# A gated cross-attention block: another order of its opening on five engines

## The chip, the cores and the metric

One core of a Trainium2 chip runs the whole program. The metric is device microseconds of one execution; the time before is a median of 490.72 us over 3 runs (490.58 to 491.27). TensorE multiplies, VectorE and ScalarE read its results out of PSUM, GpSimd works in SBUF alone, and DMA queues are fed from SyncE and ScalarE. Each engine works through its own list in order, and the engines meet at semaphores.

## The reference, cut to what matters

Eight batches of 512 rows by 256 channels go through a local attention (AFT) with a context, a feed-forward block and a second gated block.

```python
emb = x + pos_encod          # x is the context here, pos_encod the layer-normed x
q, k, v = emb @ wq + bq, emb @ wk + bk, emb @ wv + bv
w = pos_bias * (abs(i - j) < 64)
ek = exp(k - max_over_rows(k));  ew = exp(w - max_over_columns(w))
y = sigmoid(q) * (ew @ (ek * v)) / (ew @ ek)
a = layer_norm(y @ wo + bo + emb) * gamma + beta
r = layer_norm(relu(a @ w1 + b1) @ w2 + b2 + a)
x1 = x + tanh(g_xattn) * r
out = x1 + tanh(g_ffn) * gated_ffn(layernorm(x1))
```

## The kernel before, in words

Every matrix product is made of three: each operand is split into a rounded part (`_hi`, made on ScalarE) and the rest (`_lo`, made on VectorE or GpSimd), and hi·hi, lo·hi and hi·lo are added up in PSUM. So one 256x256 projection of a batch is 12 matmuls of 512 columns (`channels_out`, L1173) or 24 of 256 (`rows_out`, L1190).

The work is software-pipelined over the batches. An opening takes batch 0 to the end of its attention and into its hidden layer and prepares batch 1; seven steps (`run_steps`, L274) follow, each for three batches at different stages; a tail ends it. All orders are written out by hand, one list for each engine, and a list's next instruction waits in place if its semaphore is not there yet.

Weights come in units of 1024 columns through four staging buffers: unit 0 is keys and queries, unit 1 values and output projection, units 2 and 3 are w1, 4 and 5 w2, 6 and 7 the second block. `unit_high(u)` rounds on ScalarE, `unit_low(u)` makes the rest on VectorE or GpSimd; a unit's buffer can be loaded anew from SyncE only after its `unit_low`.

What the change touches, in the order of the opening:

- TensorE waits for the identity (L1388), then for the embedding of batch 0, turns it, and does `keys(0)` and `queries(0, 3)`; it turns the exponentials of the position bias, then those of the keys (`turn_keys`), then the masks of the far columns (L1416), and does `values(0, 3)`.
- `weigh_first` (L1297) makes the denominator, `weigh` (L1266) with part 1 the numerator. Far columns are summed by tiles: the sums go to PSUM, ScalarE rounds them (`sums_high`), VectorE makes the rest (`sums_low`), and TensorE takes them up again for the second half of the numerator. `weigh` can place other work (`between`) just ahead of the wait for these sums.
- `turn_emb(1, 1)` (L1228) turns the embedding of batch 1 between the two. ScalarE's `emb_high(1)` and a copy of it into `xk` (L1070, L1071) come ahead of `sums_high(0, 1)` (L1072) in its list.
- `fold_beta` (L1314) multiplies beta with w1, 16 products of one column, and needs w1 as loaded.
- Then the output projection, `keys(1)`, `queries(1, 3)`, the turn of the normalised rows, two quarters of the hidden layer, `values(1)`, `turn_keys(1)` and `add_hidden(0, 0)`. TensorE waits for `w_lo_done[5]` (L1448) just ahead of step 1.
- VectorE's list: `recip` (one for each of two chunks, with `sums_low(0, 1)` between them, L798), `make_y`, `make_b1`, `y_low`, `unit_low(2)`, `first_attention_sum` (L804) and so on to `keep_values(1)` (L819).
- GpSimd's list ends with `unit_low(4)`, `emb_plus_bo(1, 1)`, `unit_low(5)` (L463), `stats("mid", 0)`, `scale_a`, `stats("head", 2)` and `make_emb(pool, 2, 0)` (L467).
- ScalarE's list ends with `exp_keys(1)`, `a_high(0)`, `exp_q(1, 3)`, `normalise("head", 2, x_in)` (L1082), `hidden_high(0, 0)`, `hidden_high(0, 1)` (L1084) and `ek_high(1)`.
- SyncE's list has the loads of units 6 and 7 (L356), each behind the `unit_low` that frees its buffer, and behind them the loads for later batches.

Of the kernel before, what the change touches and what calls it, by code (L numbers as in the profile page):

```python
# [7 lines left out]
ALU = mybir.AluOpType  # L8
# [3 lines left out]
P = 128  # L12
# [16 lines left out]
NU = 8  # L29

# [12 lines left out]
def flamingo_gated_block(nc, A_x, A_ctx, A_vec, A_rows, A_far, A_pos, A_wk, A_wq, A_wv, A_wo,  # L43
# [14 lines left out]
    with ctx:  # L58
# [321 lines left out]
        def _(pool):  # L380
# [75 lines left out]
            stats("head", 1)  # L456
            emb_plus_bo(0, 0)
# [4 lines left out]
            emb_plus_bo(1, 1)  # L462
            unit_low(5)  # L463
# [3 lines left out]
            make_emb(pool, 2, 0)  # L467
            pool.wait_ge(dve_const, 4)
# [39 lines left out]
        def _(dve):  # L508
# [269 lines left out]
            unit_low(0)  # L778
            pos_max(0)
            emb_low(0)  # L780
            pos_max(1)
            head_stats(1)
            key_max(0)
            unit_low(1)
# [15 lines left out]
            make_y(0)  # L800
            make_b1()
            y_low(dve, 0)
            unit_low(2)
# [3 lines left out]
            unit_low(3)  # L807
            a_low(0)
            head_stats(2)
            sum_keys(1)  # L810
            hidden_low(0, 0)
# [5 lines left out]
            dve.tensor_scalar(gates[:, 1:2], gates[:, 2:3], 0.5, None, ALU.mult).then_inc(dve_const, 1)  # L817
            hidden_low(0, 1)
            keep_values(1)  # L819
# [81 lines left out]
        def _(act):  # L901
# [140 lines left out]
            for u in range(2):  # L1042
# [4 lines left out]
                if u == 0:  # L1047
                    unit_high(1)
            act.wait_ge(c_col_done, 1)
            act.activation(c_col, pos_nmax, ACT.Exp).then_inc(c_col_done, 1)  # L1050
            exp_keys(0)
            act.wait_ge(act_const, 1)
            exp_q(0, 3)
            act.wait_ge(far_landed, 16)
            act.wait_ge(c_col_done, 2)
            for a in range(TT):
                v = tile(far_in, TT + a, FAR)
                act.activation(v, v, ACT.Identity, scale=c_col[:, a:a + 1]).then_inc(far_masked, 1)
# [19 lines left out]
            normalise("mid", 0, res)  # L1078
            exp_keys(1)
            a_high(0)  # L1080
            exp_q(1, 3)
            normalise("head", 2, x_in)  # L1082
            hidden_high(0, 0)
            hidden_high(0, 1)  # L1084
            ek_high(1)
# [62 lines left out]
        def _(pe):  # L1148
# [165 lines left out]
            def fold_beta():  # L1314

                for k in range(DC):
                    pe.wait_ge(unit_landed[W1_UNITS[k]], unit_count(W1_UNITS[k]))
                for m in range(HC):
                    for k in range(DC):
                        last = mm(bank(3, 0)[:, m:m + 1], stage[UNIT_STAGE[W1_UNITS[k]]][:, m * P:(m + 1) * P],  # L1320
                                  vec[:, C_BETA + k:C_BETA + k + 1], m == 0 and k == 0, m == HC - 1 and k == DC - 1)
# [239 lines left out]
```

## Time and profile before

| what | value |
|---|---|
| median of 3 runs | 490.72 us |
| profiled execution | 490.83 us |
| its span, first to last instruction | 489.1 us |
| TensorE matmuls busy | 454.1 us, 93% of the span |
| VectorE | 394.0 us, 81% |
| GpSimd | 257.0 us, 53% |
| ScalarE | 239.9 us, 49% |

Busy time is an average over the whole span. Matmuls are pipelined and overlap in the rows, so the time of a group of matmuls is read from the start of its first to the start of what follows. In a timeline each row has a start and a length in us (of merged neighbours together, with their count behind the x), the engine, the line, the operation and the tile written and read; in brackets stands how long the engine was idle before it and what ended that.

### The profile page before, as it was taken

Reading aid. Unit: us, or ns where it says so; the run is one execution under the profiler, and the core shown is the slowest. Engines: PE = TensorE matmul, PEld = TensorE weight load, DVE = VectorE, ACT = ScalarE, POOL = GpSimd, SP = SyncE. Lnnn points to the kernel's source line nnn. Section 1 sums busy time; section 2 is a strip of 40 time slices with the busy share of each in tenths; the row PEclk is TensorE's granted clock in tenths of the full one; section 3 lists DMA queues with packets and bytes.
Section 4 is the critical chain, followed back from the end, with each engine's and each line's share of the span. In section 5 each row is a group of like instructions: output and inputs, shape, how many; then the busy total and the mean of one; then the engine's idle time right before and its main releaser. Section 6 shows DMA issues by size and latency. Waiting matters only on the chain.

```text
span 489.1 us, 8042 instructions
## 1 busy us (share of the span) xinstructions
PE 454.1 (93%) x3010; PEld 412.2 (84%) x3010; DVE 394.0 (81%) x725; ACT 239.9 (49%) x371; POOL 257.0 (53%) x230
## 2 busy tenths in 40 slices
PE   1889989989999999999999999999999998989776
PEld 1789789879989898989989898989889997979765
DVE  4899869987959979598959988698939974795967
ACT  2773373646265634645274644645263634446323
POOL 3657413671587536962497446952494247551510
PEclk9997999999999999999999999999999999999959
DMA  7740410012002300112002200111001100020002
GB/s 260 257 129 2 151 43 1 2 44 87 1 0 76 100 0 1 29 58 88 1 0 88 88 1 1 44 43 44 1 1 44 44 1 1 7 81 1 1 0 87
DMA packets 21894, 23.35 MB, mean 48 GB/s; under 512 B 992, under 2 KB 20960, under 8 KB 21856
## 3 DMA queue, kind: packets, MB, share of 16 engines
q1 hardware_dynamic: 20768, 21.26, 13.3%
q10 hardware_dynamic: 1088, 1.57, 0.9%
q8 instruction: 24, 0.39, 0.3%
q14 instruction: 14, 0.11, 0.1%
HBM read 18.64 MB, written 4.19 MB: 47 GB/s over the span
## 4 chain that ended last, share of the span: by engine, by line
PE 50%; issue 16%; POOL 14%; DVE 14%; ACT 4%; DMA 2%; POOLq 0%; DVEq 0%; ACTq 0%
PE ps L1150 46%; DVE y L611 4%; POOL hid_lo L219 3%; POOL xk_lo L219 2%; PE ps L1156 2%; DVE xk L679 2%; POOL a_rows L402 2%; DMA x<-in_pos 1%; PE ps L1165 1%; DVE y L608 1%; POOL ev_lo L219 1%; POOL x_beta L402 1%; DVE hid_lo L760 1%; ACT xk_hi L975 1%; DMA x_in<-in_x 1%
## 5 line engine op out<-in xcount | busy, mean ns | idle before, releaser
L1150 PE MATMUL ps<-w_hi,hid_hi 128*128 128x256 f32 x320 | 79.8, 286 | 2.7 <-DVE y L618 1.7
L760 DVE SCALAR_TENSOR_TENSOR hid_lo<-ps,neg_b,hid 128x512 fp32r<-128x512 f32 x64 | 44.1, 739 | 43.4 <-ACT hid L1020 43.4
L1150 PE MATMUL ps<-w_lo,hid_hi 128*128 128x256 f32 x320 | 78.4, 282 | 0.0
L1150 PEld LDWEIGHTS ps<-w_hi,hid_hi 128*128 128x128 f32 x320 | 60.3, 189 | 5.5 <-DVE y L618 3.7
L1150 PEld LDWEIGHTS ps<-w_lo,hid_hi 128*128 128x128 f32 x320 | 60.2, 188 | 0.2
L611 DVE RECIPROCAL y<-y 128x512 f32<-128x512 f32 x16 | 53.7, 3353 | 0.5
L1150 PE MATMUL ps<-a_hi,w_hi 128*128 128x512 f32 x128 | 50.8, 397 | 1.6 <-ACT a_hi L1003 1.6
L1014 ACT ACTIVATE hid_hi<-ps,b 128x512 fp32r<-128x512 f32 x64 | 40.5, 685 | 23.5 <-PE ps L1150 23.5
L1150 PE MATMUL ps<-a_hi,w_lo 128*128 128x512 f32 x128 | 50.8, 397 | 0.0
L1150 PE MATMUL ps<-w_hi,hid_lo 128*128 128x256 f32 x320 | 45.6, 284 | 3.5 <-DVE hid_lo L760 2.3
L219 POOL TENSOR_TENSOR ev_lo<-res,ev_hi 128x1024 fp32r<-128x1024 f32 x8 | 19.1, 2384 | 56.0 <-ACT ev_hi L963 56.0
L1150 PEld LDWEIGHTS ps<-w_hi,hid_lo 128*128 128x128 f32 x320 | 41.0, 188 | 5.1 <-DVE hid_lo L760 2.7
L1020 ACT ACTIVATE hid<-hid_hi,neg_b 128x512 f32<-128x512 f32 x64 | 42.7, 723 | 0.0
L219 POOL TENSOR_TENSOR hid_lo<-xr,hid_hi 128x1024 fp32r<-128x1024 f32 x7 | 16.8, 2403 | 37.7 <-ACT hid_hi L979 37.7
L1150 PE MATMUL ps<-a_lo,w_hi 128*128 128x512 f32 x128 | 35.1, 396 | 0.0
L1150 PEld LDWEIGHTS ps<-a_hi,w_hi 128*128 128x128 f32 x128 | 24.1, 188 | 7.0 <-issue 2.0
L402 POOL TENSOR_TENSOR a_rows<-norm,gamma_rows 128x1024 f32<-128x1024 f32 x8 | 19.8, 2471 | 19.4 <-issue 17.0
L1150 PEld LDWEIGHTS ps<-a_lo,w_hi 128*128 128x128 f32 x128 | 24.0, 188 | 6.0 <-DVE a_lo L744 0.2
L1150 PEld LDWEIGHTS ps<-a_hi,w_lo 128*128 128x128 f32 x128 | 24.1, 188 | 5.1
L1150 PE MATMUL ps<-emb_hi,w_hi 128*128 128x512 f32 x64 | 27.0, 421 | 1.2 <-ACT emb_hi L933 1.2
L1150 PE MATMUL ps<-emb_hi,w_lo 128*128 128x512 f32 x64 | 26.3, 410 | 0.0
L979 ACT ACTIVATE hid_hi<-xr 128x1024 fp32r<-128x1024 f32 x7 | 7.4, 1061 | 36.2 <-DVE xr L679 36.2
(216 smaller groups left out, 1285.9 us busy)
## 6 DMA issues: line engine op xcount, KB each, us to landing
x_in<-in_x SPq DMA_DIRECT2D x8, 512.0 KB, 4.5
emb<-in_ctx SPq DMA_DIRECT2D x8, 512.0 KB, 3.5
x_beta<-in_x SPq DMA_DIRECT2D x8, 512.0 KB, 3.6
out<-out_sb SPq DMA_DIRECT2D x7, 512.0 KB, 2.9
hid<-in_w SPq DMA_DIRECT2D x2, 512.0 KB, 4.4
x<-in_pos ACTq DMA_DIRECT2D x1, 512.0 KB, 6.4
out_sb<-in_pos ACTq DMA_DIRECT2D x1, 512.0 KB, 7.3
x<-in_w SPq DMA_DIRECT2D x1, 512.0 KB, 5.8
```

Of the source, the lines that this page charges most:

```text
L219: eng.tensor_tensor(dst, src, f32(hi), ALU.subtract).then_inc(done, 1)
L402: pool.tensor_tensor(dst.rearrange("p (a d) -> p a d", a=TT), src.rearrange("p (a d) -> p a d", a=TT), r, op).then_inc(done, 1)
L608: dve.scalar_tensor_tensor(out=tile(y, c, T), in0=tile(gate_q, c, T), scalar=1.0, in1=bank(1, c), op0=ALU.add, op1=ALU.mult).then_inc(den_ ...
L611: dve.reciprocal(tile(y, c, T), tile(y, c, T)).then_inc(recip_done, 1)
L679: dve.scalar_tensor_tensor(out=tile(dst, c, T), in0=tile(delta_buf(n), c, T), scalar=vec[:, mu + c:mu + c + 1], in1=xn_t[:, c * (T + 1):c ...
L760: dve.scalar_tensor_tensor(out=tile(hid_lo[q % 2], b, T), in0=bank(HP[q], b), scalar=neg_b1[:, m:m + 1], in1=tile(hid[q % 2], b, T), op0=A ...
L975: act.activation(tile(xk_hi, c, T), tile(xk, c, T), ACT.Copy).then_inc(xk_hi_done, 1)
L979: act.activation(xr_hi, xr_of(n), ACT.Copy).then_inc(xr_hi_done, 1)
L1014: act.activation(tile(hid_hi[q % 2], b, T), bank(HP[q], b), ACT.Relu, bias=b1[:, m:m + 1]).then_inc(hid_hi_done, 1)
L1020: act.activation(tile(hid[q % 2], b, T), f32(tile(hid_hi[q % 2], b, T)), ACT.Identity, bias=neg_b1[:, m:m + 1]).then_inc(hid_shifted, 1)
L1150: return pe.matmul(o, s, m, start=start, stop=stop, skip_group_check=True)
L1156: last = pe.transpose(bank(dst, c)[:, a * P:(a + 1) * P], src[:, D * a + c * P:D * a + (c + 1) * P], ident)
```

## The change

The lists of TensorE, VectorE, ScalarE and GpSimd for the opening are put into another order; 24 products of the identity with itself are added ahead of the first embedding; the beta products are placed between the products of the second batch's keys; and the far masks go from ScalarE to GpSimd. SyncE's list and the seven steps keep their code.

```diff
+WARM = 24
@@ GpSimd
             stats("head", 1)
+            pool.wait_ge(far_landed, 16)
+            pool.wait_ge(c_col_done, 2)
+            for a in range(TT):
+                v = tile(far_in, TT + a, FAR)
+                pool.tensor_scalar(v, v, c_col[:, a:a + 1], None, ALU.mult).then_inc(far_masked, 1)
             emb_plus_bo(0, 0)
             make_emb(pool, 1, 1)
             ev_low(0)
             low(pool, emb_lo, xk, emb_hi, emb_raw_done, 1, emb_lo_done)
             unit_low(4)
-            emb_plus_bo(1, 1)
-            unit_low(5)
             stats("mid", 0)
             scale_a(0, 0)
             stats("head", 2)
             make_emb(pool, 2, 0)
+            emb_plus_bo(1, 1)
+            unit_low(5)
@@ VectorE
             unit_low(0)
+            emb_low(0)
             pos_max(0)
-            emb_low(0)
+            dve.wait_ge(vec_landed, 16)
+            key_max(0)
             pos_max(1)
+            unit_low(1)
             head_stats(1)
-            key_max(0)
-            unit_low(1)
...
             make_y(0)
+            unit_low(2)
+            y_low(dve, 0)
             make_b1()
-            y_low(dve, 0)
-            unit_low(2)
+            unit_low(3)
             first_attention_sum()
             key_max(1)
             normalise_mid(0)
-            unit_low(3)
-            a_low(0)
-            head_stats(2)
-            sum_keys(1)
-            hidden_low(0, 0)
...
+            a_low(0)
+            head_stats(2)
+            sum_keys(1)
+            hidden_low(0, 0)
             hidden_low(0, 1)
-            keep_values(1)
+            keep_values(1, 3)
@@ ScalarE
                 if u == 0:
                     unit_high(1)
+                    exp_keys(0)
             act.wait_ge(c_col_done, 1)
             act.activation(c_col, pos_nmax, ACT.Exp).then_inc(c_col_done, 1)
-            exp_keys(0)
             act.wait_ge(act_const, 1)
             exp_q(0, 3)
-            act.wait_ge(far_landed, 16)
-            act.wait_ge(c_col_done, 2)
-            for a in range(TT):
-                v = tile(far_in, TT + a, FAR)
-                act.activation(v, v, ACT.Identity, scale=c_col[:, a:a + 1]).then_inc(far_masked, 1)
...
             normalise("mid", 0, res)
+            exp_q(1, 0)
+            a_high(0)
             exp_keys(1)
-            a_high(0)
-            exp_q(1, 3)
-            normalise("head", 2, x_in)
             hidden_high(0, 0)
             hidden_high(0, 1)
+            normalise("head", 2, x_in)
             ek_high(1)
@@ TensorE
-            def fold_beta():
...
+            def fold_beta(m):
+
+                for k in range(DC):
+                    last = mm(bank(3, 0)[:, m:m + 1], stage[UNIT_STAGE[W1_UNITS[k]]][:, m * P:(m + 1) * P],
+                              vec[:, C_BETA + k:C_BETA + k + 1], m == 0 and k == 0, m == HC - 1 and k == DC - 1)
+                return last
+
+            def keys_and_beta():
+
+                hi, lo = unit(0, 0)
+                pe.wait_ge(emb_hi_done, 2)
+                pe.wait_ge(den_read, DC)
+                pe.wait_ge(val_done, 1)
+                for k in range(DC):
+                    pe.wait_ge(unit_landed[W1_UNITS[k]], unit_count(W1_UNITS[k]))
+                m = 0
+                for k in range(DC):
+                    for c in range(DC):
+                        for r in (hi, lo):
+                            mm(bank(1, c), r[:, D * k + c * P:D * k + (c + 1) * P], tile(emb_hi, k, T),
+                               k == 0 and r is hi, False)
+                            last = fold_beta(m)
+                            m += 1
+                last.then_inc(beta_w1_done, 1)
+                pe.wait_ge(emb_lo_done, 2)
...
+                last.then_inc(k_done, 1)
@@ TensorE's list
             pe.wait_ge(ident_set, 2)
+            for _ in range(WARM):
+                mm(bank(3, 1)[:, 0:P], ident, ident, True, True)
...
             keys(0)
             queries(0, 3)
+            pe.wait_ge(ek_done, DC)
+            turn_keys(0)
             pe.wait_ge(pos_exp_done, TT)
...
-            pe.wait_ge(ek_done, DC)
-            turn_keys(0)
+            pe.wait_ge(exp_q_done, DC)
+            pe.wait_ge(w_lo_done[1], 1)
+            values(0, 3)
             pe.wait_ge(far_masked, TT)
...
-            pe.wait_ge(exp_q_done, DC)
-            pe.wait_ge(w_lo_done[1], 1)
-            values(0, 3)
             weigh_first()
-            turn_emb(1, 1)
             pe.wait_ge(ev_hi_done, 1)
             pe.wait_ge(sums_lo_done, 1)
             pe.wait_ge(tile_rows_done, 1)
-            weigh(0, 1, 2, ev_hi, ev_lo, ev_lo_done, num_done)
-            pe.wait_ge(val_done, 1)
-            fold_beta()
+            weigh(0, 1, 2, ev_hi, ev_lo, ev_lo_done, num_done, lambda: turn_emb(1, 1))
+            keys_and_beta()
             pe.wait_ge(y_hi_done, 1)
             rows_out(2, unit(1, 1), y_hi, y_lo, y_lo_done, 1, wo_done, wo_half_done)
-            keys(1)
+            queries(1, 0)
             pe.wait_ge(b1_done, 1)
-            queries(1, 3)
+            values(1, 3)
             pe.wait_ge(norm_done["mid"], TT)
             turn(2, norm, mid_turned)
...
-            pe.wait_ge(emb_lo_done, 2)
+            pe.wait_ge(exp_q_done, DC * 2)
             hidden(0, 0, 0)
             hidden(0, 1)
             pe.wait_ge(ek_done, DC * 2)
-            values(1)
             turn_keys(1)
             pe.wait_ge(w_lo_done[4], 1)
+            pe.wait_ge(val_done, 2)
             add_hidden(0, 0)
             pe.wait_ge(w_lo_done[5], 1)
```

## Rows read from the trace of the kernel before

**Rows 1.** Timeline of TensorE's matmuls (PE) in the opening and into step 1.

```profile
10.22 1.94 PE L1393 MATMUL ps<-ident,emb 128*128 128x128 f32 x8 [10.22 <-DVE emb L776]
13.37 0.77 PE L1150 MATMUL ps<-emb_hi,w_hi 128*128 128x512 f32 x1 [1.21 <-ACT emb_hi L933]
...
18.22 0.39 PE L1150 MATMUL ps<-emb_hi,w_hi 128*128 128x512 f32 x1
...
21.01 0.38 PE L1409 MATMUL ps<-ident,x 128*128 128x128 f32 x2
...
38.28 3.78 PE L1150 MATMUL ps<-vec,hid 128*128 128x1 f32 x32
42.60 0.58 PE L1150 MATMUL ps<-w_hi,ek_hi 128*128 128x256 f32 x1 [0.55 <-ACT ek_hi L997]
...
48.32 0.45 PE L1150 MATMUL ps<-emb_hi,w_hi 128*128 128x512 f32 x1
...
54.16 1.09 PE L1156 MATMUL ps<-ident,norm 128*128 128x128 f32 x8
56.04 0.47 PE L1150 MATMUL ps<-a_hi,w_hi 128*128 128x512 f32 x1 [0.78 <-ACT a_hi L1003]
...
61.73 0.28 PE L1150 MATMUL ps<-w_hi,emb_hi 128*128 128x256 f32 x1
...
70.47 0.28 PE L1150 MATMUL ps<-ew_hi,ek_hi 128*128 128x256 f32 x1
```

**Rows 2.** Stretches: length; busy PE, PEld, DVE, ACT, POOL; granted clock; DMA share, GB/s.

```profile
42.00:44.00 2.00, 1.46 (x7) 1.40 (x7) 1.87 (x3) 0.55 (x1) 2.00 (x2) 0.50 0.00 0
...
466.00:468.00 2.00, 1.03 (x4) 0.93 (x4) 0.92 (x1) 0.00 (x0) 1.92 (x3) 0.50 0.00 0
```

**Rows 3.** Timeline of GpSimd (POOL): the identity's select and one pass over 1024 columns.

```profile
1.24 0.29 POOL L440 TENSOR_SCALAR_AFFINE_SELECT ident<-ident 128x128 f32<-128x128 f32 x1 [0.24 <-POOL ident L438]
...
63.48 2.36 POOL L237 TENSOR_TENSOR emb<-x_in,emb 128x1024 f32<-128x1024 f32 x1 [2.32 <-ACT x_in L903]
```

**Rows 4.** Timeline of ScalarE (ACT) in the opening.

```profile
21.87 1.27 ACT L945 ACTIVATE gate_q<-ps,neg_bq 128x512 f32<-128x512 f32 x2
23.01 1.08 ACT L1058 ACTIVATE xr<-xr,c_col 128x68 f32<-128x68 f32 x4
...
32.99 1.03 ACT L933 ACTIVATE emb_hi<-ps 128x1024 fp32r<-128x1024 f32 x1 [0.85 <-PE ps L1156]
...
35.38 0.38 ACT L958 ACTIVATE sums_r<-ps 68x256 fp32r<-68x256 f32 x1 [0.45 <-PE ps L1150]
...
61.26 2.08 ACT L903 ACTIVATE x_in<-x_in,nmr_head,rs_head 128x256 f32<-128x256 f32 x4 [3.72 <-POOL nmr_head L397]
63.25 1.24 ACT L1014 ACTIVATE hid_hi<-ps,b 128x512 fp32r<-128x512 f32 x2
...
65.62 1.24 ACT L1014 ACTIVATE hid_hi<-ps,b 128x512 fp32r<-128x512 f32 x2
```

**Rows 5.** Timeline of VectorE (DVE) in the opening.

```profile
19.00 1.19 DVE L537 TENSOR_REDUCE neg_kmax<-ps 128x2 f32<-128x1024 f32 x1
...
29.82 1.22 DVE L583 TENSOR_TENSOR res<-ps,res 128x1024 f32<-128x1024 f32 x1
...
35.79 0.42 DVE L600 TENSOR_TENSOR sums_r<-ps,sums_r 4x256 fp32r<-4x256 f32 x1 [0.77 <-ACT sums_r L958]
...
40.24 1.22 DVE L618 TENSOR_TENSOR y<-ps,y 128x512 f32<-128x512 f32 x2
...
44.61 3.38 DVE L591 SCALAR_TENSOR_TENSOR w_lo<-hid,vec,w_hi 128x1024 fp32r<-128x1024 f32 x1
47.91 0.68 DVE L731 TENSOR_TENSOR res<-ps,emb 128x512 f32<-128x512 f32 x1
...
53.67 1.28 DVE L591 SCALAR_TENSOR_TENSOR w_lo<-hid,vec,w_hi 128x1024 fp32r<-128x1024 f32 x1
```

**Rows 6.** Timeline of TensorE in the tail: its longest idle time there.

```profile
464.22 0.36 PE L1150 MATMUL ps<-w_hi,ev_hi 128*128 128x256 f32 x1 [2.60 <-ACT ev_hi L993]
```

More of the change, by code:

```diff
@@ L1312, in weigh_first @@
                     mm(bank(1, c), sums_r[0][0:FAR, c * P:(c + 1) * P], far_c[0:FAR], False, True).then_inc(den_done, 1)
-            def fold_beta():
+            def fold_beta(m):
[8 more added lines that the diff above has]
+                pe.wait_ge(val_done, 1)
                 for k in range(DC):
                     pe.wait_ge(unit_landed[W1_UNITS[k]], unit_count(W1_UNITS[k]))
-                for m in range(HC):
+                m = 0
[8 more added lines that the diff above has]
+                pe.wait_ge(emb_lo_done, 2)
+                for c in range(DC):
                     for k in range(DC):
-                        last = mm(bank(3, 0)[:, m:m + 1], stage[UNIT_STAGE[W1_UNITS[k]]][:, m * P:(m + 1) * P],
-                                  vec[:, C_BETA + k:C_BETA + k + 1], m == 0 and k == 0, m == HC - 1 and k == DC - 1)
-                last.then_inc(beta_w1_done, 1)
+                        last = mm(bank(1, c), hi[:, D * k + c * P:D * k + (c + 1) * P], tile(emb_lo, k, T),
+                                  False, k == DC - 1)
+                last.then_inc(k_done, 1)
             def hidden(n, q, hi_count=None):
```

## The prediction

> **What bounds the kernel now.** I first looked at which engine is busy from end to end. The lines by engine give TensorE as the busiest, 93% of the span, and its waits lie almost all in the opening and in a tail that the change does not touch. So the seven steps run at TensorE's pace, and the time is, to a good approximation, the moment at which step 1 starts, 70.47 us [rows 1], plus a constant. What the change is worth is read from the opening: by how much does that first product of step 1 move?
>
> Then the opening by engine. TensorE does nothing until the first embedding at 10.22 [rows 1]. The twelve matmuls of the first keys take 4.85 us (13.37 to 18.22), the same twelve of the queries 2.79 (18.22 to 21.01) [rows 1]: a factor near two, so the keys ran mostly at 1.2 GHz and the queries at 2.4. (Here the pace tells the level; the column of the granted clock shows no fall this early.) After the 3.78 us of one-column beta products the granted clock is 0.50 [rows 2], and the 24 matmuls of the first output projection need 5.72 us, 42.60 to 48.32 [rows 1]. These two slow stretches are the places where the change could win.
>
> **The change, step by step.** All times are in the profiled execution, whose own time is 490.83 us, 0.11 above the median shown.
>
> *Identity products.* 24 products in f32; the 16 beta products show as 32 matmuls [rows 1], so these are 48. Eight 128-column ones take 1.94 us at the low clock [rows 1] and 1.09 at the high one [rows 1], so 11.6 us for all 48 if the clock never rises and 6.5 if it were high at once. They start when the identity is there, at 1.53 [rows 3]. If the clock rises after about as much work as the keys needed (4.7 us), 19 are done by then and the other 29 take 3.9: the end is 10.2, just when the embedding comes. I take no delay; the ends are 0 and 3.0 us (13.2). The first transposes then take 1.1 instead of 1.94, the keys 2.8 instead of 4.85: keys end near 15.4, 2.8 us earlier.
>
> *Front reordering.* Keys' maximum (1.19 [rows 5]) can start at 15.5 instead of 19.0 and now goes ahead of the second position maximum, of the same size: with the two small biases between them they end at 17.2 and 18.4. The second pair of position exponentials, as long as the queries' (1.27 [rows 4]), ends at 19.95, the queries' own at 21.35 behind the small one for c_col. So the values start at 21.5 and end at 24.4, as long as the queries took. The far transposes now stand behind them on TensorE. ScalarE loses 1.08 us of masks of 68 columns [rows 4]. On GpSimd the nearest rows are a 128x128 select, 0.29, below, and a two-input pass over 1024 columns, 2.36, above [rows 3]; by the first the four masks cost 1.2 us, by the second 9.4. I take 1.2, the row of nearly the same size: they stand behind the statistics of batch 1, which end near 23.1 (VectorE's unit_low(1) and statistics and GpSimd's part, 4.7 us from 18.4 on), and so end at 24.3, beside the values. If they were slower, the far transposes and all that follows would wait. Then far_c (25.0 to 25.6) and normalising batch 1 (2.08, as for batch 2 [rows 4]) lie in front of the first sums on ScalarE, which are rounded by 28.05; with sums_low the weighing of the values starts at 28.5 instead of 29.82 [rows 5]. Of 2.8 us won, 1.3 are left (ends 0 and 2.8).
>
> *The transposes of batch 1 move into the numerator.* This is the first new wait. Weighing from 28.5 on (1.22 [rows 5]), rounding on ScalarE (1.03, as [rows 4]) and one GpSimd pass (2.36 [rows 3]) put ev_lo at 33.3. Four matmuls of tile sums and four of near products, 0.12 each, end at 34.0 and 34.4, and the eight transposes (1.0) at 35.35. But ScalarE's queue is unchanged: the embedding's rounding (1.03) and a copy of the same size stand ahead of the second sums [rows 4]. Before, the transposes were early (the rounding began at 32.99) and ScalarE was through with both when the sums came at 35.38. Now the rounding cannot start before 35.4, the copy ends at 37.35, the sums' rounding (0.38) at 37.75, and VectorE's sums_low runs then instead of at 35.79 [rows 5]. Behind it in VectorE's queue stands the second reciprocal: from sums_low to y is 4.45 us, and y takes 1.22 [rows 5], so y is complete at 43.4, 1.95 later than 41.46. TensorE stands idle from 35.35 to 38.2, 2.9 us.
>
> *Beta products between keys.* From sums_low's end to the end of the numerator were 2.05 us (36.21 [rows 5] to 38.28 [rows 1]); now TensorE gets there at 40.2. Eight groups of one key matmul and two beta products: 3.78 us [rows 1] if the keys' columns hide under the beta loads, 3.78 + 8/12 of 2.79 = 5.6 in sequence; I take 4.7, and 0.95 for the last four key matmuls: 45.85. y is rounded by 44.5 and y_low, behind unit_low(2) on VectorE, ends at 45.85. unit_low(2) itself took 3.38 us beside GpSimd's unit_low(5), the same work on the other half 1.28 [rows 5]; the moved GpSimd work takes that 2.1 away. The projection at 2.4 GHz takes 24 x 0.12 = 2.9 us (half the columns of the queries' matmuls, 0.23 each), 45.9 to 48.8. The first attention sum can start at 47.55, against 47.91 [rows 5]. So three effects of 2 us each have nearly cancelled: 0.4 us are won (ends: 1.2 lost, 0.4 won, by the beta pace).
>
> *Queries and values ahead of the turn.* From that sum to the turn of the normalised rows were 6.25 us (47.91 [rows 5] to 54.16 [rows 1]), by VectorE, GpSimd and ScalarE; now these rows are ready at 53.8. But TensorE does queries and values, 2.85 us each, from 48.8 to 54.5 and so turns them at 54.5, 0.3 later than before; the first hidden product is at 56.35 instead of 56.04, and 5.69 us later (61.73 before [rows 1]) both first quarters are done: 62.05.
>
> *The second new wait decides.* Before, normalising batch 2 stood ahead of the hidden roundings on ScalarE (61.26), and unit_low(5) had long been done on GpSimd. Now normalising stands behind both hidden roundings, and on GpSimd make_emb, the adding of bo and unit_low(5) stand behind it, in that order; TensorE waits for unit_low(5) just ahead of step 1. From the end of the hidden products: 0.2 to ScalarE, 2.4 for the second rounding (63.25 to 65.62) and 2.08 for normalising [rows 4], 66.8; then three GpSimd passes of 2.36 [rows 3], less the small overlap of back-to-back ones, 7.0: 73.85, and step 1 at 73.95. That is 3.5 us later than 70.47 (ends 3.0 and 4.8). Values already done (2.9 us) only lengthen TensorE's idle time: turned keys end at 63.6, add_hidden waits for the kept values until 66.7, runs to 69.65, and 4.3 us are idle. Behind unit_low(5) SyncE also holds the loads of unit 7, x_beta and x of batch 3; their readers come in the middle of step 1, so 0, else one landing.
>
> *The clock after that wait.* In the tail an idle time of 2.60 us [rows 6] was followed by a granted clock of 0.50 in the stretch from 466 on [rows 2]. Here 3.1 and 4.3 us of idling stand close together, so step 1 begins at 1.2 GHz. What such a stretch costs: the projection lost 5.72 - 2.9 = 2.8 us, the keys 2.06 [rows 1]. I take 2.5, with 0 and 2.8 as ends. [...]
>
> Sum: 3.5 + 2.5 = 6.0 us, so 496.8 for the profiled execution and 496.7 against the median.
>
> **The rivals.** *The gap at 35.35 drops the clock too.* Its 2.9 us exceed the 2.60 of [rows 6]; against it, 2.0 us of products lie near on both sides. The numerator's second half then costs 1.5 more, and the interleaved keys and the projection up to 2.3 more: 498.2 to 500.5. Chance 0.22.
>
> *The clock holds or its loss is covered* at step 1: 3.5 us alone, 494.2. For it speaks that add_hidden lies between the two idle times. Chance 0.16.
>
> *The identity products don't raise the clock,* so the change doesn't do its first part: the first transposes start near 13, keys stay slow, some 4 us more than my sum, 500.5. Chance 0.05.
>
> *Faster.* The clock stays at 2.4 GHz through the opening and the waits behind GpSimd don't bind: 2.06 + 2.8 = 4.9 us won, 485.8. The place is TensorE's wait for unit_low(5). It decides where that ends before 70.47, so the hidden products would have to end by 58.6, 3.4 earlier than I have them. The early gain would have to pass the second sums whole. Chance 0.10.
>
> *The effects cancel* within 1 us (about 0.2%, what a measurement can tell from no change): 490.7, chance 0.05.
>
> **How the numbers follow.** My forecast has 0.42; the rest is above. Slower is the forecast and the three cases of the same sign, 0.85; same 0.05; faster 0.10. The range leaves out the two cases at or below no change and a little at the top: from the smallest shift of step 1 at full clock less some error (2.1 us, 492.8) to 500.6.
>
> **What would show it.** Right: twelve key matmuls in about 2.8 us ending near 15.5; TensorE idle for 2 to 3 us between the turned embedding and the second sums; y near 43; projection at 0.12 us per matmul; TensorE's last wait of the opening ended by GpSimd's w_lo; half clock at the start of step 1. Wrong: step 1 starting before 70.5, or unit_low(5) done before add_hidden ends.

## The result, and the profile after

The changed kernel takes 505.1 us (median; 500.2 to 506.2) against 490.65 us for the kernel before in the same comparison: a ratio of 1.0272, with a 95% interval of 1.0214 to 1.0329. The direction was forecast and the size was not: 14.4 us slower instead of 6.0, and outside the range. The profiled execution is the fastest one, 500.18 us. So there are two misses: 3.4 us in the execution that can be looked into, and 4.9 more in the median. A ratio leaves out executions that are more than 1.5% above the fastest of their kernel; among all kernels here that touches e1 alone, two of whose four executions fall out.

TensorE's timeline after, to be laid beside [rows 1]:

```profile
1.57 8.03 PE L1152 MATMUL ps<-ident 128*128 128x128 f32 x48 [1.57 <-POOL minus_one L444]
10.47 0.66 PE L1418 MATMUL ps<-ident,emb 128*128 128x128 f32 x4 [0.86 <-DVE emb L782]
11.91 0.66 PE L1418 MATMUL ps<-ident,emb 128*128 128x128 f32 x4 [0.79 <-DVE emb L782]
13.89 0.80 PE L1152 MATMUL ps<-emb_hi,w_hi 128*128 128x512 f32 x1 [1.32 <-DVE w_lo L600]
...
18.15 0.40 PE L1152 MATMUL ps<-emb_hi,w_hi 128*128 128x512 f32 x1
...
37.51 1.04 PE L1158 MATMUL ps<-ident,emb 128*128 128x128 f32 x8
41.35 0.58 PE L1152 MATMUL ps<-ew_hi,ev_hi 128*128 128x256 f32 x1 [2.81 <-DVE sums_r L606]
...
44.60 0.40 PE L1152 MATMUL ps<-emb_hi,w_hi 128*128 128x512 f32 x1
...
49.93 1.18 PE L1152 MATMUL ps<-emb_lo,w_hi 128*128 128x512 f32 x4
50.95 0.28 PE L1152 MATMUL ps<-w_hi,ek_hi 128*128 128x256 f32 x1
...
53.83 0.39 PE L1152 MATMUL ps<-emb_hi,w_hi 128*128 128x512 f32 x1
...
59.51 1.04 PE L1158 MATMUL ps<-ident,norm 128*128 128x128 f32 x8
...
66.07 1.10 PE L1152 MATMUL ps<-a_lo,w_hi 128*128 128x512 f32 x4
...
71.76 0.55 PE L1152 MATMUL ps<-w_hi,hid_hi 128*128 128x256 f32 x1 [2.77 <-issue]
...
78.87 0.58 PE L1152 MATMUL ps<-ew_hi,ek_hi 128*128 128x256 f32 x1 [2.61 <-POOL w_lo L423]
```

The page's line of TensorE's busy time is all but the same share as before:

```profile
PE 462.7 (93%) x3058; PEld 420.2 (84%) x3058; DVE 394.1 (79%) x725; ACT 239.0 (48%) x367; POOL 257.0 (52%) x234
```

The loss is not seen in it; it is in the timeline. Both new waits are there, at 41.35 behind the second sums and at 78.87 behind GpSimd. Step 1 starts 8.40 us later than the 70.47 of [rows 1]; from there to the end it is 421.31 us (500.18 - 78.87) against 420.36 before. So the opening holds nearly all of the loss, as the prediction had read it.

The granted clock of four stretches after (columns as in [rows 2]; the third value from the end is the clock, 1.00 for 2.4 GHz and 0.50 for 1.2):

```profile
14.00:16.00 2.00, 2.00 (x5) 1.61 (x6) 2.00 (x2) 0.00 (x0) 0.74 (x1) 0.50 1.09 384
...
42.00:44.00 2.00, 2.00 (x11) 2.00 (x11) 1.97 (x2) 2.00 (x3) 1.10 (x2) 0.50 0.03 8
...
72.00:74.00 2.00, 2.00 (x10) 2.00 (x11) 1.40 (x2) 0.56 (x1) 2.00 (x1) 0.50 0.00 0
...
80.00:82.00 2.00, 2.00 (x12) 1.98 (x12) 0.00 (x0) 0.00 (x0) 0.00 (x0) 0.57 0.93 318
```

Four pieces of the opening run at half clock: most of the keys, the second half of the numerator, most of the added hidden part, and the start of step 1.

VectorE after, beside [rows 5]:

```profile
9.28 2.58 DVE L782 TENSOR_TENSOR emb<-x_in,emb 128x512 f32<-128x512 f32 x2 [0.47 <-ACT x_in L910]
11.78 2.06 DVE L600 TENSOR_TENSOR w_lo<-hid,w_hi 128x1024 fp32r<-128x1024 f32 x1
...
18.42 1.22 DVE L543 TENSOR_REDUCE neg_kmax<-ps 128x2 f32<-128x1024 f32 x1 [2.32 <-PE ps L1152]
...
20.06 1.21 DVE L555 TENSOR_REDUCE pos_nmax<-out_sb 128x2 f32<-128x1024 f32 x1
21.18 1.21 DVE L600 TENSOR_TENSOR w_lo<-hid,w_hi 128x1024 fp32r<-128x1024 f32 x1
22.32 1.40 DVE L519 BATCH_NORM_STATS2 st_head<-x_in 128x6 f32<-128x256 f32 x4
...
31.67 1.23 DVE L589 TENSOR_TENSOR res<-ps,res 128x1024 f32<-128x1024 f32 x1
...
45.31 1.28 DVE L624 TENSOR_TENSOR y<-ps,y 128x512 f32<-128x512 f32 x2
46.51 1.28 DVE L597 SCALAR_TENSOR_TENSOR w_lo<-hid,vec,w_hi 128x1024 fp32r<-128x1024 f32 x1
...
70.45 1.22 DVE L565 TENSOR_TENSOR res<-ps,bv_rows 128x1024 f32<-128x1024 f32 x1
```

VectorE waits 2.32 us for the keys, and the second position maximum, the second unit's lower half and the statistics stand behind that wait. The weighing of the values starts at 31.67: predicted was 28.5, before it was 29.82.

GpSimd after, beside [rows 3]; the first row is the first of four selects of the position bias, which end at 14.74, the second holds the far masks, the last three are the passes behind batch 2's normalising:

```profile
8.82 1.05 POOL L452 TENSOR_SCALAR_AFFINE_SELECT x<-x 128x1024 f32<-128x1024 f32 x1 [0.78 <-DMA x<-in_pos]
...
25.91 1.73 POOL L462 TENSOR_SCALAR xr<-xr,c_col 128x68 f32<-128x68 f32 x4
...
71.80 2.38 POOL L238 TENSOR_TENSOR emb<-x_in,emb 128x1024 f32<-128x1024 f32 x1 [5.34 <-ACT x_in L910]
74.14 2.37 POOL L403 TENSOR_TENSOR emb<-emb,bo_rows 128x1024 f32<-128x1024 f32 x1
76.48 2.33 POOL L423 TENSOR_TENSOR w_lo<-out_sb,w_hi 128x1024 fp32r<-128x1024 f32 x1
```

### The profile page after: what moved, and what is told of

It reads as the page before. It is cut to its first block, busy times and chain, and to the rows that moved or that the text cites. A ratio compares the mean times of both kernels' runs of the same rounds, so it can differ in the third digit from the quotient of the medians.

```text
span 498.5 us, 8137 instructions
## 1 busy us (share of the span) xinstructions
PE 462.7 (93%) x3058; PEld 420.2 (84%) x3058; DVE 394.1 (79%) x725; ACT 239.0 (48%) x367; POOL 257.0 (52%) x234
## 4 chain that ended last, share of the span: by engine, by line
PE 52%; POOL 15%; issue 15%; DVE 10%; ACT 4%; DMA 2%; POOLq 0%; DVEq 0%; ACTq 0%
PE ps L1152 48%; DVE y L617 4%; POOL hid_lo L220 3%; PE ps L1158 3%; POOL xk_lo L220 2%; DVE xk L685 2%; POOL a_rows L403 1%; PE ps L1167 1%; DVE y L614 1%; POOL ev_lo L220 1%; POOL x_beta L403 1%; POOL emb L403 1%; DMA x<-in_pos 1%; ACT x_in L910 1%; ACT xk_hi L982 1%
## 5 line engine op out<-in xcount | busy, mean ns | idle before, releaser
L1152 PE MATMUL ps<-w_hi,hid_hi 128*128 128x256 f32 x320 | 81.2, 289 | 5.4 <-issue 2.8
L1152 PE MATMUL ps<-w_lo,hid_hi 128*128 128x256 f32 x320 | 79.6, 285 | 0.0
L1152 PEld LDWEIGHTS ps<-w_hi,hid_hi 128*128 128x128 f32 x320 | 61.4, 192 | 8.3 <-issue 3.7
L1152 PEld LDWEIGHTS ps<-w_lo,hid_hi 128*128 128x128 f32 x320 | 61.3, 191 | 0.2
```

Of the source, the lines that this page charges most:

```text
L1152: return pe.matmul(o, s, m, start=start, stop=stop, skip_group_check=True)
```

## The experiments

Sixteen kernels, each against the kernel before on the same chip (its medians there 490.9 to 491.3). They are told in the order of the opening's waits, not in the order of their names.

**The two new waits, undone one at a time.** e1 takes only GpSimd's list back to its old order:

```diff
             unit_low(4)
+            emb_plus_bo(1, 1)
+            unit_low(5)
             stats("mid", 0)
...
             make_emb(pool, 2, 0)
-            emb_plus_bo(1, 1)
-            unit_low(5)
```

> The changed kernel with GpSimd's adding of bo and unit_low(5) back ahead of the statistics of the middle; nothing else. Theory (queues): TensorE's wait before step 1 goes, step 1 starts where add_hidden ends, 76.1 us in the changed kernel's profile instead of 78.87, and without an idle stretch there the clock does not fall a second time: profiled about 3.5 us under the changed kernel's 500.18, and the other runs shift by 3 to 6. unit_low(2) and y_low on VectorE can lose up to 2 us beside GpSimd again. Rival (clock alone): the idle time only moves elsewhere, under 1 us is won.

Measured: 501.8 us (495.4 to 505.2), ratio 1.0136 [1.0075, 1.0196]: 3.3 less than the change by the medians, 6.7 by the ratios. Step 1 waits for GpSimd no more. The profiled execution is this version's slowest, 505.22, and shows where an execution of that length loses its time. The granted clock there:

```profile
44.00:48.00 4.00, 4.00 (x18) 3.62 (x17) 4.00 (x3) 2.42 (x3) 3.10 (x3) 0.51 0.01 4
...
56.00:60.00 4.00, 4.00 (x16) 3.61 (x16) 1.43 (x3) 0.00 (x0) 0.00 (x0) 0.50 0.00 0
```

From 44 on the interleaved keys and the projection run at half clock with TensorE busy throughout; in the changed kernel's profile these ran at 2.4 GHz.

e2 puts the transposes back where they were in TensorE's list:

```diff
             weigh_first()
+            turn_emb(1, 1)
...
-            weigh(0, 1, 2, ev_hi, ev_lo, ev_lo_done, num_done, lambda: turn_emb(1, 1))
+            weigh(0, 1, 2, ev_hi, ev_lo, ev_lo_done, num_done)
```

> The changed kernel with the turning of batch 1's embedding back ahead of the numerator. Theory (queues): ScalarE's rounding and copy are done before the second sums, the 2.81 us of idle TensorE at 38.6 to 41.35 go, y comes about 3 us earlier (43.6 instead of 46.59), the numerator's second half runs at full clock (1.2 us), and step 1 starts 3 to 4.5 us earlier: 496 to 497 in a profile. Rival: the beta pace or unit_low on VectorE takes up what is won, under 1 us.

Measured: 498.9 us (497.7 to 500.0), ratio 1.0159 [1.0136, 1.0183], 6.2 less. The profiled execution is e2's slowest, 499.98, and hardly shorter than the changed kernel's. The wait is gone and y is complete at 44.29 instead of 46.59, as expected; but the front is 0.90 later there (the weighing starts at 32.57), and the clock falls in the interleaved keys instead (0.50 from 46 to 52): keys and projection take 12.29 us (41.04 to 53.33) against 9.23 in the changed kernel's profile (44.60 to 53.83). So the 6.2 stand on the medians alone. e3 makes both edits:

> Both edits together. Theory: the two waits are in series, so the gains add: 6 to 8 us under the changed kernel, near 493, still above the kernel before because of the front reordering (values and GpSimd's masks ahead of the far transposes, 1.8 us late at the weighing of the values). Rival (clock alone): the gains do not add.

Measured: 495.1 us (492.1 to 497.2), ratio 1.0065 [1.0029, 1.0101], 10.0 less. The two waits lie one behind the other, and neither hides the other: the gains of e1 and e2 sum to 9.5 by the medians and to 12.2 by the ratios. Whether they add exactly is not shown; e1's four executions lie too far apart for that. Undoing GpSimd's move has a price of its own: beside GpSimd's passes `unit_low(2)` and `y_low` take 3.21 and 3.39 us on VectorE in e3, instead of 1.28 and 1.23 in the changed kernel.

**The same two waits, put into the kernel before, each alone.** The edits the other way round; e11 touches GpSimd's list and then ScalarE's:

```diff
-            emb_plus_bo(1, 1)
-            unit_low(5)
             stats("mid", 0)
...
             make_emb(pool, 2, 0)
+            emb_plus_bo(1, 1)
+            unit_low(5)
...
-            normalise("head", 2, x_in)
             hidden_high(0, 0)
             hidden_high(0, 1)
+            normalise("head", 2, x_in)
```

and e12 TensorE's:

```diff
             weigh_first()
-            turn_emb(1, 1)
...
-            weigh(0, 1, 2, ev_hi, ev_lo, ev_lo_done, num_done)
+            weigh(0, 1, 2, ev_hi, ev_lo, ev_lo_done, num_done, lambda: turn_emb(1, 1))
```

> The kernel before with the second new wait alone: GpSimd's emb_plus_bo(1,1) and unit_low(5) behind make_emb(2,0), head 2's normalise behind the hidden layer. Theory (that wait is a fixed price in series): step 1 waits for GpSimd's w_lo and starts near 73 to 75 (70.47 before), 493.5 to 496. Rival (in the order of before GpSimd has the room, and the wait costs only beside the other parts of the change): under 1 more, 490.5 to 491.9.

> The kernel before with the first new wait alone: the transposes of batch 1's embedding between the two halves of the numerator. Theory (2.8 idle, then half clock in the numerator's second half): y done at 44.5 to 45.5 (41.46 before), partly taken up by slack at the projection's lower y, 492.5 to 494.5. Rival (the queue behind it has that much slack): under 1 more, 490.5 to 491.9.

Measured: e11 495.5 us, ratio 1.0086 [1.0066, 1.0107], 4.2 more than before; e12 496.7 us, ratio 1.0125 [1.0094, 1.0156], 5.4 more, above what even the theory allowed. TensorE's last wait of the opening in e11:

```profile
72.57 0.58 PE L1150 MATMUL ps<-ew_hi,ek_hi 128*128 128x256 f32 x1 [5.06 <-POOL w_lo L422]
```

The granted clock of a stretch behind it:

```profile
74.00:76.00 2.00, 2.00 (x12) 1.95 (x11) 0.00 (x0) 0.03 (x1) 0.00 (x0) 0.50 1.01 349
```

2.10 us of the 4.5 of that profiled execution (495.32 against 490.83) are step 1's later start; the other 2.39 lie behind it, where step 1 starts at half clock (the row above). In e12, TensorE's wait for the second sums:

```profile
39.92 0.58 PE L1150 MATMUL ps<-ew_hi,ev_hi 128*128 128x256 f32 x1 [2.81 <-DVE sums_r L600]
```

and VectorE's last pass on y:

```profile
43.89 1.22 DVE L618 TENSOR_TENSOR y<-ps,y 128x512 f32<-128x512 f32 x2
```

y is done at 45.1, 3.65 later than the 41.46 from [rows 5], and none of it is taken up on the way. More comes in: TensorE idles another 1.56 us for the lower y at 50.72, where the kernel before has no wait, and step 1 starts at 75.85, 5.38 later.

**The clock.** Products of the identity with itself in the idle places keep TensorE at work and change nothing else (e5, on the changed kernel; `fill(o, n)` is n such products into a free bank):

```diff
             last.then_inc(emb_turned, 1)
+            fill(bank(3, 1), 4)
...
+            def turn_and_fill():
+                turn_emb(1, 1)
+                pe.wait_ge(val_done, 1)
+                fill(bank(3, 1), 12)
-            weigh(0, 1, 2, ev_hi, ev_lo, ev_lo_done, num_done, lambda: turn_emb(1, 1))
+            weigh(0, 1, 2, ev_hi, ev_lo, ev_lo_done, num_done, turn_and_fill)
...
+            fill(bank(1, 0), 12)
             pe.wait_ge(val_done, 2)
             add_hidden(0, 0)
+            fill(bank(1, 0), 12)
             pe.wait_ge(w_lo_done[5], 1)
```

> The changed kernel with TensorE's idle stretches filled: 4 products of the identity behind the first transposes, 12 behind the turning of batch 1's embedding, 12 ahead of add_hidden's wait and 12 behind add_hidden; they write PSUM that nobody reads any more, and every real wait stays. Theory (the clock takes what lies beyond the waits, and differs from run to run): the granted clock stays 1.00 up to step 1, step 1 starts near 77 us, the time is 497 to 499 and the runs lie within 2 us, against 500 to 506 for the changed kernel. Rival (the scatter is transfers or GpSimd's port): the median stays above 502 and the scatter too.

Measured: 497.55 us (497.54 to 498.01), ratio 1.0129 [1.0113, 1.0145]: 7.5 less than the change, and the scatter has gone. TensorE's fillers behind the added hidden part, and its last wait:

```profile
73.76 2.84 PE L1152 MATMUL ps<-ident 128*128 128x128 f32 x24
77.95 0.38 PE L1152 MATMUL ps<-ew_hi,ek_hi 128*128 128x256 f32 x1 [1.35 <-POOL w_lo L423]
```

The granted clock where step 1 starts in e5:

```profile
78.00:80.00 2.00, 2.00 (x17) 2.00 (x18) 0.00 (x0) 0.10 (x1) 0.00 (x0) 1.00 0.36 96
```

Step 1 still starts at 77.95, but at 2.4 GHz. The waits are the same, so by the medians 7.5 of the 14.4 us go with the clock at the filled gaps (four of the fillers stand behind the first transposes, so a part of this can be the front's). The other 7 are not the waits and the order alone. The clock did not stay at 1.00 up to step 1, as was expected; in the profiled execution it falls with TensorE busy throughout, at the end of the interleaved keys:

```profile
46.00:48.00 2.00, 2.00 (x7) 1.71 (x8) 1.56 (x4) 0.00 (x0) 0.00 (x0) 0.50 0.00 0
```

It is 0.50 until 52, and keys and projection take 12.27 us (40.63 to 52.90) against 9.23 in the changed kernel's profile. So about 3 us of what is left are the clock again, as far as one execution shows.

**The identity products of the change,** left out on the changed kernel (e4), and on e9, the fastest version below (e15):

```diff
-WARM = 24
+WARM = 0
```

> The changed kernel without the 24 identity products. Theory: in the changed kernel's profile the clock had fallen again before the first keys, so nothing is lost without them: keys end within 0.5 us of 18.15 us and the time is within 1 us of the changed kernel's. Rival (the products work in the other runs): the median rises by 2 us or more, as the keys' 2 us are then always lost.

> The same version without the identity products. Theory (they bring the keys to 2.4 GHz, but what is behind the keys waits for VectorE and GpSimd): keys of batch 0 end near 18.2 instead of 15.5, time 0 to 1 more than 489.8. Rival (they are worth what the prediction counted, 1.3 and more): 491 to 492.5.

Measured: e4 503.2 us, ratio 1.0245 [1.0209, 1.0281], within the scatter of the change; e15 489.8 us, ratio 0.9987 [0.9972, 1.0002], against 489.8 with them. They are worth nothing measurable in either order. e9, which has the products and the front as before, shows why; VectorE's timeline there:

```profile
9.34 1.29 DVE L777 TENSOR_TENSOR emb<-x_in,emb 128x512 f32<-128x512 f32 x2 [0.47 <-ACT x_in L905]
...
16.09 1.21 DVE L550 TENSOR_REDUCE pos_nmax<-out_sb 128x2 f32<-128x1024 f32 x1
17.22 1.40 DVE L514 BATCH_NORM_STATS2 st_head<-x_in 128x6 f32<-128x256 f32 x4
...
18.95 1.19 DVE L538 TENSOR_REDUCE neg_kmax<-ps 128x2 f32<-128x1024 f32 x1
```

Here the keys began at 12.55 and at 2.4 GHz, and their maximum still starts at 18.95. VectorE's list decides that: its first position maximum waits 2.06 us for GpSimd's selects, the embedding's lower half stands behind it (TensorE waits 1.58 us for it within the keys), and from 13.82 on the list is full. In e15, with keys from 13.29 on at the pace of the lower clock, the keys' maximum starts at 18.86.

**The front.** On e3, with both waits undone, the front's lists were put back as before, masks included (e7). VectorE's list:

```diff
             unit_low(0)
+            pos_max(0)
             emb_low(0)
-            pos_max(0)
+            pos_max(1)
+            head_stats(1)
             dve.wait_ge(vec_landed, 16)
             key_max(0)
-            pos_max(1)
             unit_low(1)
-            head_stats(1)
```

> Both waits undone, and the front as before the change: masks on ScalarE, values behind the far transposes, VectorE's first part in the old order; identity products and interleaving stay. Theory: values ahead of the far transposes and four GpSimd masks (1.73 us) behind the statistics of batch 1 cost 1 to 2 us at the weighing of the values, so the median is 493 to 494, 1 to 2 under the run of both. Rival: the front is neutral, within 0.7.

Measured: 493.2 us (492.3 to 494.5), ratio 1.0040 [1.0028, 1.0052]: 1.9 less than e3. Which part of it costs was then tried on e9: the masks alone on GpSimd (e13), the change's order on VectorE, ScalarE and TensorE with the masks left on ScalarE (e14, the last diff the other way round), all of it (e16). The masks' part:

```diff
             stats("head", 1)
+            for a in range(TT):
+                v = tile(far_in, TT + a, FAR)
+                pool.tensor_scalar(v, v, c_col[:, a:a + 1], None, ALU.mult).then_inc(far_masked, 1)
...
-                act.activation(v, v, ACT.Identity, scale=c_col[:, a:a + 1]).then_inc(far_masked, 1)
```

> The version with both waits undone, the front as before and the kept values early (489.8), with the far masks alone moved to GpSimd. Theory (the masks hold up GpSimd, whose first pass for the embedding of batch 1 and ev_low stand behind them, and far_c behind them on ScalarE): weighing of values 0.5 to 1.5 later than 29.9, 490.3 to 491.5. Rival (GpSimd has that room, the order is the cost): within 0.5 of 489.8.

> The same version with the front's new order on VectorE, ScalarE and TensorE, the masks left on ScalarE behind the queries' exponentials. Theory (as the prediction had it, an earlier keys' maximum brings the values and their weighing forward): weighing of values near 28.5 to 29.5, 488.0 to 489.5. Rival (the order costs, since statistics and the second unit's lower half now stand behind the keys' maximum): 490.5 to 491.8.

> The same version with the whole front of the changed kernel, order and masks. Theory (the front costs 1.9, as between the two versions without the early kept values): 491.3 to 492.3, the sum of the two parts measured beside it. Rival (with the idle stretch before the hidden layer gone, the front's cost is hidden): 489.5 to 490.3.

Measured: e13 489.15 us, ratio 0.9965 [0.9946, 0.9984]; e14 491.5 us (487.8 to 494.0), ratio 1.0003 [0.9984, 1.0022]; e16 491.9 us (488.9 to 494.4), ratio 1.0008 [0.9984, 1.0031]. The order costs about 1.7 us and scatters; the masks show no cost in the medians. VectorE's timeline in e14:

```profile
19.23 1.23 DVE L538 TENSOR_REDUCE neg_kmax<-ps 128x2 f32<-128x1024 f32 x1 [2.69 <-PE ps L1152]
...
20.87 1.21 DVE L550 TENSOR_REDUCE pos_nmax<-out_sb 128x2 f32<-128x1024 f32 x1
...
31.81 1.23 DVE L584 TENSOR_TENSOR res<-ps,res 128x1024 f32<-128x1024 f32 x1
```

VectorE waits 2.69 us for keys that ran at 1.2 GHz (the granted clock is 0.50 from 12 to 17), with 1.21 of position maximum and 1.40 of statistics standing ready behind the wait. In the old order these lie ahead of it and fill it. So the new order can pay only where the keys come early. Whether they do goes with the landing of the position bias, on which GpSimd's selects start. The profiles of all kernels here, by front:

| front | selects start | keys' maximum | weighing of the values |
|---|---|---|---|
| new: changed kernel, e1, e2, e4, e14, e16 | 8.82 to 9.27 | 18.42 to 19.95 | 31.67 to 33.21 |
| new: e3, e5, e6 | 9.91 to 11.04 | 15.70 to 15.85 | 28.96 to 29.12 |
| old: before, e7 to e13, e15 | 8.70 to 10.91 | 18.77 to 19.31 | 29.13 to 30.26 |

e3's rows, to be laid beside those of the changed kernel:

```profile
9.91 1.50 POOL L452 TENSOR_SCALAR_AFFINE_SELECT x<-x 128x1024 f32<-128x1024 f32 x1 [1.94 <-DMA x<-in_pos]
...
15.73 1.23 DVE L543 TENSOR_REDUCE neg_kmax<-ps 128x2 f32<-128x1024 f32 x1 [0.98 <-PE ps L1152]
...
28.99 1.23 DVE L589 TENSOR_TENSOR res<-ps,res 128x1024 f32<-128x1024 f32 x1
```

Against the 29.82 of the kernel before, the new front wins 0.7 to 0.9 us where the selects start late and loses 1.9 to 3.4 where they start early; with the old one the weighing varies by less than 1.2 us. How often an execution has which is not shown, since each kernel was profiled once. From the keys' maximum to the weighing it is 13.25 us in the new order with the masks on GpSimd and 12.58 with them on ScalarE (e14); in the old order it is 9.88 with them on GpSimd (e13) and 10.82 without (e9). So the masks' move costs 0.7 us in the new order and wins 0.9 in the old, which the medians are too coarse to show.

**The beta products,** back in one block ahead of the projection, with keys(1) behind it (e6 on e3, e8 on e7):

```diff
-            keys_and_beta()
+            for m in range(HC):
+                last = fold_beta(m)
+            last.then_inc(beta_w1_done, 1)
             pe.wait_ge(y_hi_done, 1)
             rows_out(2, unit(1, 1), y_hi, y_lo, y_lo_done, 1, wo_done, wo_half_done)
+            keys(1)
             queries(1, 0)
```

> Both waits undone (as in the run of both), and the beta products back in one block ahead of the output projection, the second keys behind it. Theory: interleaved they make a stretch of some 6 to 10 us in which the clock falls or does not come back, so without it the median falls 1 to 3 us, to 492 to 494. Rival: interleaving is neutral or good, the time rises by up to 3 us, as the projection runs at half clock again.

> All of it undone but the identity products, the moves of unit_low on VectorE and of queries and values ahead of the turn. Theory: the gains add, 490 to 492, level with the kernel before or a little under it. Rival: above 493.

Measured: e6 497.3 us, ratio 1.0128 [1.0098, 1.0157], 2.2 more than e3; e8 497.4 us, ratio 1.0130 [1.0103, 1.0157], 4.3 more than e7. Beside the rest of the change this part is good. Without it, TensorE comes early to the projection's lower y, which VectorE has not made: the change put `unit_low(2)` ahead of `y_low`, and beside GpSimd's passes the two end at 47.19 in e6; before, `y_low` ended at 44.68. Whether the interleaving wins anything with `y_low` in its old place was not tried. e6's TensorE at that place:

```profile
47.25 1.22 PE L1152 MATMUL ps<-w_hi,ek_lo 128*128 128x256 f32 x4 [3.21 <-DVE ek_lo L220]
```

**A third wait.** e3 and e7 still idle 2.77 us ahead of the added hidden part, as the change does at 71.76: its operands are there, but the kept values, which free the bank it writes, stand behind both lower hidden parts on VectorE (70.45 after). This wait is new with the change too, which brings the values into that bank. e9, on e7, moves them ahead on VectorE, and the four small operations on gates and biases between the two lower hidden parts:

```diff
             normalise_mid(0)
+            keep_values(1, 3)
             a_low(0)
...
             hidden_low(0, 1)
-            keep_values(1, 3)
```

> Both waits undone, the front as before, and VectorE's keep_values(1,3) moved ahead of the lower parts of the hidden layer, for which add_hidden waited 2.77 in that version's profile. Theory (a third wait, with the clock falling behind it): add_hidden starts without idle, the clock stays at 2.4 GHz there, step 1 starts near 69.0 to 70.0 (73.14 without the edit), time 489 to 490.5, under the 490.9 of the kernel before. Rival (keep_values in front delays the lower hidden parts, and turn_keys(1) waits for them instead): step 1 at 72 to 73.5, time 492 to 493.5.

> The same with the identity products kept going until the embedding is there (28 instead of 24 ahead, four behind the first transposes). Theory (clock): keys of batch 0 at 2.4 GHz end near 15.5 instead of 18.2, but VectorE's weighing of values and the eviction behind it take most of that; 1 to 2 less than the version without, 487.5 to 489.5. Rival (the opening is bound by VectorE and GpSimd, not by the keys): no difference within 0.5.

Measured: e9 489.8 us (488.8 to 492.5), ratio 0.9972 [0.9953, 0.9990], 3.4 less than e7; e10, with 28 instead of 24 identity products and four more behind the first transposes, 489.7 us, ratio 0.9974 [0.9958, 0.9990], so nothing more. TensorE in e9, from the added hidden part to step 1:

```profile
66.26 0.36 PE L1152 MATMUL ps<-w_hi,hid_hi 128*128 128x256 f32 x1
...
70.19 0.36 PE L1152 MATMUL ps<-ew_hi,ek_hi 128*128 128x256 f32 x1 [0.81 <-issue]
```

The added hidden part follows the turned keys at once, and step 1 starts at 70.19. This execution is one of e9's three longest, 492.16: the clock falls once more within step 1 (0.56 from 102 to 104). e9, e10 and e13 beat both kernels, by 1.5 to 1.9 us against the kernel before; e13's 0.6 over e9 is inside the scatter.

## Why the prediction was right or wrong

**Right: the second new wait.** From the end of the hidden products to step 1 it had 11.9 us; by the profile it is 11.87 (67.0, four products of 0.23 from 66.07 on, to 78.87). Queries and values ahead of the turn (5.68 us from 53.83 to 59.51, predicted 5.7), the projection (2.88, predicted 2.9) and unit_low(2) at 1.28 came out too. So did the premise that the time is the start of step 1 plus a constant: from there to the end it is 419.9 to 420.4 us in the 13 profiles whose clock is up from the start of step 1 on, and 421.3 to 422.8 in the five where it is down within step 1 (the change, e2, e4 and e11 near its start, e9 at 102).

**Wrong: "Identity products", and with it "Front reordering".** This is the step that made the profiled execution miss. The two were to bring the weighing of the values to 28.5; it came at 31.67, 3.17 later. The products themselves did what was said: they end at 9.60, and the transposes behind them run at full pace, four in 0.66. But the embedding came in halves, at 10.47 and 11.91, since VectorE's adding took 2.58 us instead of the 1.29 seen in e9. In this execution GpSimd's selects start at 8.82 and lie over it; in e9 the position bias lands later and they start at 10.87, behind it. The Trainium skill (SBUF — State Buffer, Who interferes with whom) says that a VectorE operation with two inputs in SBUF and a GpSimd operation that reads SBUF shut each other out; both rows agree. After gaps of 0.86, 0.79 and 1.32 us the clock fell again, the keys ended at 18.15 instead of 15.4, and of 2.8 us won 0.07 were left. The prediction had one profile to go by, in which the selects start at 10.91; where they start that late in the new front, the weighing comes at 28.96 to 29.12 (e3, e5, e6). The chain of the reordering was right, 13.0 us from the keys' maximum to the weighing against 13.25, but it was judged with early keys only. With late ones it puts VectorE's spare work behind the wait, and 1.3 us won became 1.9 lost. The masks were mis-sized too, 1.73 instead of 1.2.

**Wrong in its bounds: "Transposes of batch 1 move into the numerator".** The wait was right, 2.81 us of idling against 2.9. That the rest of the change "nearly cancelled" it was not: undone in the changed kernel it gives 6.2 us back by the medians (e2), and alone in the kernel before it costs 5.4 (e12), because what it delays is the chain that sets the end. The clock fell in that gap (0.50 from 42 to 44), and the numerator's second half took 3.25 us instead of 2.05. The Trainium skill (TensorE: Matmul & The Clock Gate, HAM oscillation) tells of a kernel whose clock is down again after each wait between its bursts of matmuls; the waits of its example are longer, and here one of 2.81 us was enough. This is what the first rival said, to which the prediction gave 0.22. That its 498.2 to 500.5 holds the profiled execution is luck: its other part, slow interleaved keys and a slow projection, did not come there, and the 3.2 us of the front, which it did not have, stand in its place.

**Mis-sized: "Beta products between keys".** A group of one key product and two beta products takes 0.67 us at full clock, not 0.59, and the whole block 6.35 instead of 5.65. **Mis-sized the other way: "The clock after that wait",** 0.95 us instead of 2.5 in this execution, though 2.39 in e11.

The sum for the profiled execution: step 1 was predicted at 73.95 and came at 78.87, 4.92 later: 3.2 from the front, 1.2 from the clock in the numerator, 0.7 from the beta block, and small terms of -0.2. Less 1.55 on the clock behind step 1 this is 3.4, the miss of 500.18 against 496.8.

**Not in the prediction at all: that the time would scatter.** The other executions are 3 to 6 us longer than the profiled one, and longer the lower their mean granted clock: 500.2 us at 0.976, 503.6 at 0.973, 504.9 at 0.969, 505.3 at 0.963, 506.2 at 0.956. The prediction priced the clock as one fixed term, at step 1. But where a fall reaches the interleaved keys, it can run on through them and the projection with TensorE busy throughout (e1, 44 to 60). With the gaps filled the executions lie within 0.5 us (e5), although the clock falls there too; why it then falls alike in each is not shown. Which of the changed kernel's stretches were slow in its executions of 505 is not shown, since none of them was profiled; e1's of 505.22 is the nearest, so the cause of the 4.9 us in the median stays open in part.

By medians, undone in this order, the 14.4 us come apart as 10.0 for the two new waits with what the clock makes of them (e3), 1.9 for the front's order (e7) and 3.4 for the third wait (e9), less the 0.9 that is left over: e9 is a little faster than the kernel before (1.5 us against the one measured beside it). What wins this, the rest of the change or e9's own move of the kept values, was not taken apart; the beta products between the keys are worth 4.3 us in e7 (e8).

## What to carry to other kernels

In a list written by hand, work that is ready must not stand behind a wait that its own engine could have spent on it: each of the three waits, and the front's loss, is one operation put behind another that comes late. Two waits on one chain can both count even where each looks covered by itself, so try each alone in the kernel before. A price read from one profile holds for that execution: here one landing, some 2 us earlier, turned a gain into a loss. And an idle stretch of TensorE of nearly 3 us cost more than its length here, as a median and as scatter; a few useless products in it show what the clock made of that gap, but look at the granted clock behind it too, for it can fall there instead (e5).

## What the runs showed of the hardware that was not expected

The granted clock can fall with no idle stretch near ahead of it. In e3's interleaved keys, with TensorE busy from 35.44 on (columns as above):

```profile
41.00:43.00 2.00, 2.00 (x10) 1.80 (x9) 2.00 (x1) 0.78 (x1) 2.00 (x2) 0.50 0.00 0
```

And the landing of one transfer, some 2 us earlier or later from execution to execution, doubles the time of a VectorE operation that has nothing to do with it (2.58 us in the changed kernel, 1.29 in e9), through GpSimd's work on what landed.
